# Eight-headed attention: sign sums in pieces, statistics spread over the steps, the first tile's weights turned by TensorE, the rest of the keys weighed by VectorE

## The reference

```python
# eight heads of 64, context of 154 keys
sim = jnp.einsum('bihd,bjhd->bhij', q, k) * SCALE
attn = jax.nn.softmax(sim, axis=-1)
out = jnp.einsum('bhij,bjhd->bihd', attn, v).reshape(B, Nq, H * D)
x = x + out @ Wo + bo
# feed-forward with sign weights
h = jnp.concatenate([x, -x], axis=-1)          # of the layer-normed x
h = jax.nn.relu(s0 * (h @ sign(k0))) * 2
h = jax.nn.relu(s1 * (h @ sign(k1))) * 2
x = x + s2 * (h @ sign(k2))
```

## Time and profile before

| | us |
|---|---|
| median of 3 runs | 991.59 |
| the profiled execution | 993.34 |
| its span | 991.6 |
| first to last instruction of the headed attention | 691.8 to 821.6 |
| feed-forward, first matmul to the end | 822.6 to 991.6 |

### The profile page before, as it was taken

One profiled execution on the slowest core, in us unless ns is written; L12 is line 12 of the kernel. 1 busy time (PEld: TensorE's weight loads), 2 busy tenths in 40 slices (PEclk: granted clock), 3 DMA queues, 4 the chain that ended last, 5 costly groups with the idle time before them and its releaser, 6 DMA issues. The chain is left out here.

```text
span 991.6 us, 23089 instructions
## 1 busy us (share of the span) xinstructions
PE 831.8 (84%) x9188; PEld 539.6 (54%) x9188; DVE 777.6 (78%) x1402; ACT 650.9 (66%) x1153; POOL 376.6 (38%) x372
## 2 busy tenths in 40 slices
PE   1387779798579889999968999998799878999997
PEld 0122223232246646555635776766687665778786
DVE  7999989934568989887768999996889966667443
ACT  4579689887568635544228888886798656656431
POOL 1042444322136413000027888886345622224220
PEclk9998889897769989999979999999999899999999
DMA  5402414050041030000040000000565340000000
GB/s 153 85 2 33 54 29 59 8 79 1 16 155 44 1 114 26 2 1 1 1 154 22 3 3 3 4 2 2 128 108 91 72 78 2 1 12 12 12 22 32
DMA packets 60554, 40.36 MB, mean 41 GB/s; under 512 B 44880, under 2 KB 56862, under 8 KB 59296
## 3 DMA queue, kind: packets, MB, share of 16 engines
q1 hardware_dynamic: 57696, 36.27, 17.1%
q10 hardware_dynamic: 2752, 2.62, 0.9%
HBM read 18.56 MB, written 2.10 MB: 21 GB/s over the span
## 5 line engine op out<-in xcount | busy, mean ns | idle before, releaser
L589 ACT ACTIVATE t_pT<-t_sc 128x1536 f32<-128x1536 f32 x96 | 136.7, 1454 | 29.0 <-PE t_sc L696 28.8
L269 POOL TENSOR_SCALAR_AFFINE_SELECT t_pT<-t_pT 128x512 f32<-128x512 f32 x64 | 75.1, 1194 | 168.5 <-ACT t_pT L589 168.5
L696 PE MATMUL t_sc<-t_qk 32*128 32x512 f16 (+3 forms) x1152 | 89.3, 365 | 46.8 <-DMA t_qk<-t_sin_parts 26.4
L696 PEld LDWEIGHTS t_sc<-t_qk 32*128 32x128 f16 x1152 | 37.0, 99 | 106.9 <-issue 52.3
L717 PE MATMUL t_ot<-t_pT,t_v 128*17 128x512 f32 (+3 forms) x768 | 81.9, 538 | 11.1 <-DVE t_ou L433 5.0
L2798 POOL TENSOR_SCALAR_AFFINE_SELECT r_att<-r_att 128x1024 f16<-128x1024 f16 x64 | 68.7, 1098 | 25.4 <-DVE r_att L2847 25.4
L2016 PE MATMUL c_pso<-ck_VO,c_pT 128*128 128x256 f16 x480 | 60.0, 287 | 14.7 <-DVE x L1863 14.7
L2016 PEld LDWEIGHTS c_pso<-ck_VO,c_pT 128*128 128x128 f16 x480 | 48.9, 103 | 23.8 <-issue 14.1
L1928 ACT ACTIVATE c_pt<-c_pss,c_mx 128x154 f32<-128x154 f32 x128 | 48.3, 403 | 13.2 <-DVE c_mx L1836 13.2
L2300 ACT ACTIVATE m_sg<-m_psg 128x512 f32<-128x512 f32 x32 | 19.1, 596 | 56.5 <-PE m_psg L2343 56.4
L2364 PE MATMUL m_acc<-gw_down,m_hp 128*128 128x256 f16 x384 | 47.2, 273 | 2.4 <-DVE m_hp L2256 2.0
(11 more groups left out here) (620 smaller groups left out, 2374.1 us busy)
## 6 DMA issues: line engine op xcount, KB each, us to landing
t_qk<-t_cos_parts SPq DMA_DIRECT2D x24, 128.0 KB, 5.3
t_qk<-t_sin_parts SPq DMA_DIRECT2D x24, 128.0 KB, 6.8
x<-in_x ACTq DMA_DIRECT2D x4, 512.0 KB, 6.0
out_x<-x SPq DMA_DIRECT2D x8, 256.0 KB, 2.1
r_rcos<-in_ret_cos SPq DMA_DIRECT2D x1, 1280.0 KB, 8.3
r_rsin<-in_ret_sin SPq DMA_DIRECT2D x1, 1280.0 KB, 10.6
t_qk<-t_cos_parts SPq DMA_DIRECT2D x16, 64.0 KB, 2.7
gw_raw<-in_gateT SPq DMA_DIRECT2D x1, 1024.0 KB, 7.8
```

Of the source, the lines that this page charges most:

```text
L269: last = g.affine_select(out=blk, in_=blk, compare_op=ALU.is_ge, fill=0.0, base=0, pattern=[[0, 4], [1, P]], channel_multiplier=-1)
L589: a.activation(pT[:, at:at + 3, :].rearrange("p a s -> p (a s)"), sc[s % 2][:], ACT.Exp, scale=CURVE * CURVE / math.sqrt(2 * DH)).then_inc ...
L696: last = t.matmul(sc[s % 2][:, 512 * k + at:512 * k + at + w], qk[r, g % 3, 1, of_k, P * i:P * i + P], qk[r, g % 3, 0, of_q, q0:q0 + w], s ...
```

## The change

In order of the code: the sums of the sign weights (`mixture`) come in 16 pieces of 512 elements in place of 4 instructions of 2048, two a step from step 6 to 13, the second of each step behind `part_low` of that step (`parted`). The eight expansions come two a step (steps 2 to 5). GpSimd no longer weighs the last 26 keys: VectorE does it right behind its own multiplication, in `weigh`. The weights of tile 0 are turned by TensorE, as those of the last tile; their output comes in step 1, its addition in step 2. VectorE's small works are gathered in `beside(s)`, which stands behind `x_low` and ahead of `part_low`, `add` and `p_low`; the six statistics of `opening` are spread over steps 1 to 4 and their `spread` goes to step 5. `turn_p` stands ahead of `project`, and the third `high_p` behind `exps(s, 1)`.

```diff
-            def weigh_rest(t):
...
             for s in STEPS:
-                weigh_rest(s - 1)
-                if s == 2:
+                if s == 5:
                     opening.power(g, 2)
                 signs.on_gpsimd(g, own, s)
+                if MIX_FROM <= s < MIX_FROM + 2 * signs.PIECES:
+                    signs.mixture(g, 2 * (s - MIX_FROM))
+                    g.wait_ge(parted, s - 1)
+                    signs.mixture(g, 2 * (s - MIX_FROM) + 1)
...
                     v.tensor_tensor(pn[:, q, 0:NH, :], pt[:, q, :, 0:P], ...).then_inc(main_weighed, 1)
+                    rest = pn[:, q, NH:SLOTS, :].rearrange("p g (h k) -> p (g h) k", k=32)[:, :, 0:REST]
+                    v.tensor_tensor(rest, pt[:, q, :, P:CTX], ...).then_inc(rest_weighed, 1)
...
+            def beside(s):
+                if s == 0:
+                    signs.scales(v)
+                if s in (1, 2):
+                    opening.statistic(v, own, 2 * s + 8)
+                    opening.statistic(v, own, 2 * s + 9)
+                if s in (3, 4):
+                    opening.statistic(v, own, s + 11)
+                    signs.on_vector(v, s - 3)
+                if s == 5:
+                    opening.spread(v, own, 2)
...
+                if s in (16, 17):
+                    rows.low(v, own, s - 14)
...
                 x_low(s + 2)
+                beside(s)
                 part_low(s - 1)
-                add(s - 3)
+                if s == 2:
+                    add(0)
+                if s > 3:
+                    add(s - 3)
                 for j in range(3):
                     p_low(s - 1, j)
...
             for s in STEPS:
                 score(s + 1)
+                for j in range(3):
+                    turn_p(s - 1, j)
                 project(s + 2)
                 turn_x(s + 3)
-                for j in range(3):
-                    turn_p(s - 1, j)
-                output(s - 2)
+                if s == 1:
+                    output(0)
+                if s > 2:
+                    output(s - 2)
```

More of the change, by code:

```diff
@@ L1779, in flat, with turned, landings @@
             return a.rearrange("p s k -> p (s k)")
+        def turned(t, j):
+            return (pso, psq, pso)[j][:] if t == 0 else pss[:, (3, 4, 0)[j]]
+        def landings(t):
+            return t // 2 + t % 2
         def bank(t, k):
@@ L1788, in _ @@
             signs.load(sp, ins)
-            for t in range(LAST):
-                sp.wait_ge(parted, t + 1)
+            for t in range(1, LAST):
+                sp.wait_ge(parted, t)
                 wait(sp, out_ready, t - 1)
@@ L1863, in add @@
                     v.scalar_tensor_tensor(x[:, t, :], pso[:, 0:D], 1.0 / XSCALE, x[:, t, :], ALU.mult, ALU.add).then_inc(x_done, 1)
+            def beside(s):
[9 more added lines that the diff above has]
+                    opening.spread(v, own, 2)
+                if s == 6:
+                    opening.offsets(v, 2)
+                if s in (7, 8):
+                    v.wait_ge(x_done, 2 * s - 12)
+                    rows.statistics(v, own, 2 * s - 14, 2 * s - 12)
+                if s == 9:
+                    rows.spread(v, own, 0)
+                if s in (10, 11):
+                    v.wait_ge(x_done, 2 * s - 14)
+                    rows.statistics(v, own, 2 * s - 16, 2 * s - 14)
+                if s == 11:
+                    rows.offsets(v, 0)
+                if s in (12, 13):
+                    rows.low(v, own, s - 12)
+                if s == 14:
+                    rows.spread(v, own, 1)
+                if s == 15:
+                    rows.offsets(v, 1)
+                if s in (16, 17):
+                    rows.low(v, own, s - 14)
             for s in STEPS:
@@ L1932, in part_high @@
             def part_high(t):
-                if inside(t) and t < LAST:
+                if inside(t) and t not in BY_PE:
                     q = t % 2
@@ L1951, in _ @@
                 part_high(s - 1)
-                for j in range(3):
-                    high_p(s - 1, j)
+                high_p(s - 1, 0)
+                high_p(s - 1, 1)
                 exps(s, 1)
+                high_p(s - 1, 2)
                 exps(s, 2)
@@ L1995, in turn_p @@
             def turn_p(t, j):
-                if t == LAST:
-                    b, s0, s1 = GROUPS[j]
+                if t in BY_PE:
+                    s0, s1 = GROUPS[j]
                     if j == 0:
                         t_.wait_ge(main_weighed, t + 1)
+                    if j == 1 and t == 0:
+                        t_.wait_ge(q_copied, 3)
                     if j == 2:
                         t_.wait_ge(rest_weighed, t + 1)
+                        if t == 0:
+                            t_.wait_ge(p_split, 1)
                     for k in range(s0, s1):
-                        last = t_.transpose(pss[:, b, P * (k - s0):P * (k - s0) + P], pn[:, t % 2, k, :], ident)
+                        last = t_.transpose(turned(t, j)[:, P * (k - s0):P * (k - s0) + P], pn[:, t % 2, k, :], ident)
                     last.then_inc(p_turned, 1)
```

104 lines of the change are left out of this document (40 added, 64 removed).

## The result

The changed kernel takes 994.62 us in the median, the kernel before 992.43 beside it on the same chip (20 runs each); the ratio is 1.0028, 95% interval 1.0016 to 1.0041. The forecast was +8.15 us, measured are +2.2 (by the medians) to +2.8 (by the ratio). The sign was right, the size three to four times too large. The profiled execution lasts 994.57, its span 992.8.

A forecast was written before the change was run, and what follows sets the result against it. TensorE was taken to fill steps 5 to 9, VectorE steps 10 to 13, and a chain of engines to set the end. -1.8 by step 14, +1.25 and +8.7 gave +8.15 us: 999.7 us, range 988 to 1003.

The forecast's parts named there:

- start of step 5: VectorE before step 5: new weighings and expansion waits, less a moved spread and filled waits for ScalarE; -0.7 us.
- steps 5 to 13: Middle of the headed attention: nine VectorE steps, extras and port waits total 67.2 us against 68.29; -1.1 us.
- steps 14 and 15: Spread, new weighing and a last piece come ahead of the addition of tile 11, one wait is filled; +1.25 us.
- the end: Outputs 14 and 15: rows.low ahead of the addition makes TensorE wait twice and its clock fall; +8.7 us.
- 5.4 a step: VectorE's work in one step without waits, 5.11 plus 0.28 us for weighing the last 26 keys.
- Waits 1.3 in steps 7 to 13: VectorE waits for GpSimd's pieces at the port: 0.25 for the first, 1.05 us for the second, each step.
- needs at most its 6.57 a step: TensorE's share of a step in steps 5 to 13, with each of these steps forecast longer than 6.57 us.
- By the alternation above about 1.8: Before step 5: VectorE's waits for GpSimd's expansions, taking turns at the port, cost about 1.8 us.
- The first: Rival: the new instruction keeps the port, no piece costs more than 0.25; total +0.15, 991.7 us; chance 0.17.
- The third: Rival: alternation as forecast, but the end or the start 3 to 4 us cheaper; 996 us; chance 0.15.
- The second: Rival: port kept, early output 0 worth 2 to 4 us, TensorE's clock stays up at the end; 985.4; chance 0.11.
- The fourth: Rival: VectorE waits for both pieces in full and more for the expansions; 6 us more, 1005; chance 0.07.

The follow-up runs named there:

- after: The changed kernel itself, as measured and profiled against the kernel before: 994.62 us, ratio 1.0028.
- e2_before_tail: The kernel before with rows.low of steps 16 and 17 ahead of part_low and the addition: 1002.26 us, ratio 1.0087.
- e4_whole_sums: The changed kernel with the sums whole again, four of 2048 elements in steps 10 to 13: 1000.05 us, ratio 1.0079.
- e3_tiny_sums: The changed kernel with each of the 16 pieces of the sums computing 8 elements in place of 512: 991.09 us, ratio 0.9986.
- e11_power_in_step: The changed kernel with GpSimd's power for the statistics between the first and second piece of step 10: 997.05 us, one run.
- e10_small_works_behind: The changed kernel with all of VectorE's small works behind part_low, the addition and p_low again: 989.56 us, ratio 0.9967.
- e6: As e1, with VectorE's weighing of the last 26 keys behind the first of the two last maxima: 987.82 us, ratio 0.9936.
- e7: As e1, with both pieces of a step started behind the weighing of the last 26 keys: 983.52 us, ratio 0.9890.
- e12: As e9, with the spread of step 14 behind the addition of tile 11 again: 980.51 us, ratio 0.9881.
- e1: The changed kernel with rows.low of steps 16 and 17 behind the addition and p_low again: 987.29 us, ratio 0.9950.
- e8: As e1, with TensorE's turns of the feed-forward's row tiles ahead of the outputs in steps 14 to 16: 982.62 us, ratio 0.9890.
- e9: The changed kernel with the edits of e1, e7 and e8 together: 979.09 us, ratio 0.9863.
- e5_gpsimd_weighs: As e1, with the last 26 keys weighed by GpSimd again, ahead of the first piece: 984.58 us, ratio 0.9910.

## Why the prediction was wrong, step by step

| term | forecast | measured |
|---|---|---|
| start of step 5 | -0.7 | -1.9 |
| steps 5 to 13 | -1.1 | -5.45 |
| steps 14 and 15 | +1.25 | +1.15 |
| the end | +8.7 | +8.9 |
| sum | +8.15 | +2.7 |

**The end** was right in place, size and both waits: 3.02 and 2.61 (forecast 3.0 and 2.6). In its 8.9 are 0.4 at the barrier that the sum did not have (TensorE idle 1.89 there, 1.47 before); its cause is open. That the clock fell behind both waits was in part luck: five kernels have these two waits, three of them (after, e2_before_tail, e4_whole_sums) show both falls, e3_tiny_sums the first alone, e11_power_in_step none.

**Steps 14 and 15** came out in size. That the order causes it is not shown: e10_small_works_behind undid it and won nothing, by way of the clock.

**"Steps 5 to 13 ... -1.1" is the step that failed**, by 4.35, and in four places, each read in the trace of after, the first in that of e3_tiny_sums as well:
- The step of VectorE without waits. "5.4 a step" was 5.19 (5.85 - 0.66, e3_tiny_sums). I had read it from step 7, whose reciprocal started 0.49 behind the maximum; in step 8, not read, it is 0.38. And a wait printed as 0.34 costs 0.42 from start to start, since it stands where 0.08 of overlap would be. Nine times 0.2: 1.8.
- "Waits 1.3 in steps 7 to 13": right in kind, 1.19 in six of the steps, but 0.23 in step 11, where the power stands between the pieces, as the order of GpSimd's stream could have told me. 9.1 was forecast, 6 x 1.19 + 0.23 = 7.4 came: 1.7.
- "1.4 in step 6": 0.8; the expansions ran mostly beside maxima, which took their usual 1.17. 0.6.
- "`spread` 1.4": the one of step 5 has six instructions, not seven, and took 1.07. 0.3.

Together 4.4, against 4.35. Each error had the same sign, so none made up for another. That TensorE "needs at most its 6.57 a step" and each step is longer was wrong too, though the sum did not use it: steps 5, 6 and 11 took 6.32, 6.07 and 6.14.

**The start.** "By the alternation above about 1.8" for the expansions: VectorE's instructions with two inputs in SBUF show 0.14 + 0.06 there (1.36 and 1.28 in place of 1.22). The other kernels that share this start reach step 5 in 30.1 to 32.5 us, those of the old start in 32.1 and 33.4. Most of this scatter goes with the granted clock of step 0, which no edit touches: 1.00 in before, after, e6, e7 and e12, 0.76 to 0.78 in e1, e8 and e9 (30.6 to 30.9 us), 0.50 to 0.54 in e2, e4 and e11 (33.4, 32.5 and 32.4). Kernels of like clock differ by 1.9 (after, before) and by 0.9 to 1.0 (e4 or e11, e2), so the forecast of -0.7 was 0.2 to 1.2 short, and no single cause within it was isolated.

**The rivals.** The first (the new instruction keeps the port) fell: 1.32. By that literal rule of the Trainium skill (SBUF — State Buffer, Who interferes with whom) it would have been 0.36 throughout. The trace disagrees again as in the earlier trace rows: the waiting GpSimd instruction came between two VectorE instructions back to back. The third, "the end or the start 3 to 4 us cheaper: 996", comes near the time, but it was mostly the middle that was cheaper. The second fell with its conditions: both waits came with a low clock, and steps 7 and 8 took 7.04. The fourth fell too: the main weighing and the new instruction together waited 1.19 and not the 2.2 of both pieces in full.

## What to carry to other kernels

A small work that waits for a third engine must not stand ahead of the instruction for which TensorE waits: here two of them cost some 8.5 us (the 8.9 of the end without the 0.4 at the barrier) and took back all that the rest of the change had gained (6.2), and 3.1 of it were TensorE's slow clock (1.66 and 1.40). Place GpSimd's two-input work beside VectorE's maxima, `x_low` and statistics (L820), none of which waited in e7_pieces_under_maxima, and not so that it queues between two port instructions (1.32 us where 0.37 was needed). When a term is a step times nine, read the step in two places: 0.2 us wrong becomes 1.8. Before a difference of 1 or 2 us between two traces is put down to an edit, compare the granted clock of the stretches that the edit does not touch.

## What the runs showed of the hardware that I had not expected

- The clock behind a wait is not fixed by its length. Outputs took 5.10 behind waits of 1.76 (e6_rest_later), 2.31 and 2.50, but 3.44 behind 3.01 and 2.60 in e11_power_in_step, with a granted clock of 1.00, and 3.44 behind 1.75 and 1.76. Output 13 was slow behind each wait of 4.52 or 4.53, but it took 4.91 (e3_tiny_sums) to 6.34 (e5_gpsimd_weighs), so one wait cost 1.5 to 2.9. Windows over the two outputs of e11_power_in_step:

```profile
814.74:818.10 3.36, 3.36 (x32) 3.02 (x33) 2.02 (x5) 0.00 (x0) 0.00 (x0) 1.00 0.02 5
821.00:824.30 3.30, 3.30 (x30) 2.83 (x30) 0.00 (x0) 0.00 (x0) 0.00 (x0) 1.00 0.00 0
```

- The 6.57 that I took as TensorE's share of a step is not its share. Outputs follow one another every 6.25 without a wait, in e3_tiny_sums (734.48, 740.72, 746.97) and in the kernel before as well (726.07, 732.32, 738.56, 744.81). The window of the earlier trace rows was cut by VectorE's steps, and TensorE did more than five steps' work in it: 385 matmuls, where the five steps after have 360.

- The wait for the port falls on tiny instructions (2.16 above), and also on one with a single tile as input: in e4_whole_sums the pair of L852, which reads one tile of x, took 3.27 in place of 0.73, and in e7_pieces_under_maxima 1.43 and 1.48. The Trainium skill (SBUF — State Buffer, Who interferes with whom) counts `tensor_scalar` among those that can meet GpSimd at the port; the trace agrees with that.
